# First expert layer: 20 of 32 token tiles go through 48 slot tiles sorted by expert, 12 tiles stay dense

## The chip, the core and the metric

The program runs on one core of a Trainium2 chip. Its engines work side by side and meet at semaphores: PE (TensorE, matmuls; its weight loads are listed as PEld), DVE (VectorE), ACT (ScalarE), POOL (GpSimd) and SP (SyncE, which here only issues DMAs). The metric is the device time of one execution in microseconds, the median over runs. Lower is better.

## The reference, cut to what matters

Six layers follow each other on `x` of 128 x 32 tokens with 128 features. The change concerns the third, the first expert layer. A token's result there is the sum over its two best experts, so the work that the mathematics asks for is 2 of 8 experts for each token:

```python
logits = x @ router_weight                      # 4096 tokens, E = 8 experts
probs = softmax(logits); top_p, top_i = top_k(probs, 2)
top_p = top_p / sum(top_p)
# an expert takes at most cap = ceil(4096 * 2 / 8 * 1.25) = 1280 entries, later ones are dropped
fc1 = gelu(xt @ moe_w1[e])                      # 128 -> 256
fc2 = fc1 @ moe_w2[e]                           # 256 -> 128
moe_out[token] += fc2 * top_p                   # for its two experts
return h1 + moe_out
```

## The kernel before

Tokens lie in 32 tiles of 128 rows (one token in each partition). `k.X` holds the running residual, all in SBUF. Each layer is a stage with its own program for each engine, and all engines meet between stages.

The projection stage (`stage_projection`) ends the attention ahead of the experts: it adds to `k.HID`, normalises rows into `xr`, transposes them into `k.LT` (on ACT, with the layer norm's weight and bias), and makes router logits. POOL adds `k.HID` to `k.X` there (L1583).

The expert stage (`stage_experts_two`) is dense. PE takes blocks of four tiles, and for each block all eight experts: 64 units numbered n = 8 b + e. A unit is `h` (L1654: 2 matmuls of 512 columns), gelu on ACT (L1687), `y` (L1664: 8 matmuls of 128 columns, for four tiles and two halves of the 256), and on DVE four additions into `k.X` scaled with the token's share of that expert, which is zero for the six experts that it doesn't use (L1750). PE runs one `h` ahead of `y`, and y banks are four deep: `y(n)` waits for the additions of unit n-3.

While PE begins, DVE works out the shares in a chain of small operations, each waiting for the one before: softmax, first and second best expert, the number of each entry within its expert (`ranks` on PE, prefix sums over the tiles on DVE, L1729 and L1730), and the drop at 1280. The last of them is L1737; `y(3)` waits for it through the semaphore `known`. After each block DVE takes the row statistics for the next layer norm (L1755, L104). SP and POOL have next to nothing to do in this stage.

The last stage of the program (`stage_routed_experts`) already routes another expert layer, which has one expert for each token, 512 hidden features and a gate. DVE works out a slot for each token (ops up to L2067), POOL stores the normalised rows at their slots in the DRAM tensor `slot_rows` with 32 indirect DMAs (L1853), SP loads 40 slot tiles one at a time into six buffers (L1818), and for each of them PE transposes (L1892), does 8 matmuls (L1900) and 4 more (L1909), ACT does gelu and two copies, DVE copies the expert's first weights (L2013), and POOL stores the result at the tokens' places with an indirect DMA (L1859). PE and DVE read the number of the tile's expert from SBUF into a register of their sequencer (`value_load`, L1905 and L2011).

Of the kernel before, what the change touches and what calls it, by code (L numbers as in the profile page):

```python
# [33 lines left out]
ST = NT + 8  # L34
EPS = 1e-5
# [1441 lines left out]
def stage_projection(nc, k, w, wb, wr):  # L1477
    W = 4
    NG = NT // W
    with ExitStack() as ctx:  # L1480
# [3 lines left out]
        def sem(name):  # L1484
# [7 lines left out]
            "normed", "transposed", "copied", "logits_made", "logits_copied", "x_summed"))  # L1492
        block = ctx.enter_context(nc.Block())
# [4 lines left out]
        def span(g):  # L1498
            return slice(W * g, W * g + W)

        @block.tensor
        def _(pe):
# [6 lines left out]
            def turn(g):  # L1509
                wait(pe, copied, g - 1)  # L1510
                for i in range(W):
                    pe.wait_ge(normed, W * g + i + 1)
                    m = pe.transpose(pT[g % 2][:, i * P:(i + 1) * P], xr[g % 2][:, i, :], k.ident[:, :])
                m.then_inc(turned, 1)
# [35 lines left out]
        def _(dve):  # L1550
# [11 lines left out]
            def norm(g):  # L1562
# [4 lines left out]
                for i, t in enumerate(tiles(g)):  # L1567
                    dve.tensor_scalar(xr[g % 2][:, i, :], k.HID[:, t, :], k.MV[:, t, 0:1], k.RSTD[:, t:t + 1],
                                      ALU.subtract, ALU.mult).then_inc(normed, 1)
# [26 lines left out]
def stage_experts_two(nc, k, low, down, w1, w2):  # L1596
# [4 lines left out]
    NB = NT // TB  # L1601
    with ExitStack() as ctx:
# [12 lines left out]
        pr, tmp, oh, sel = (sb(n, [P, NT, E]) for n in ("probs", "tmp", "onehot", "selected"))  # L1615
        acc = [sb(f"prefix{i}", [P, NT, E]) for i in range(2)]
        pH = (k.bank[0:2], k.bank[2:4])
        WAYS = 4
        pY = k.bank[4:8]
        pR, pC = k.bank[7][:, 0:NT * E], k.bank[7][:, NT * E:2 * NT * E]  # L1620
        ones_set, chain, exped, sel_ready, ranked, shifted, known = (sem(n) for n in (
            "ones_set", "chain", "exp_done", "selected_ready", "ranks_made", "shifted", "shares_known"))
        h_made, gelued, y_made, added, stats = (sem(n) for n in ("h_made", "gelu_done", "y_made", "added", "stats"))
        ctx.callback(leave_stale, k, sems, scope)
        block = ctx.enter_context(nc.Block())

        def blocks(eng, body):

            body(0, True, False)
            with eng.Fori(0, NB - 2) as i:  # L1630
                body(i + 1, False, False)
            body(NB - 1, False, True)

        @block.sync
        def _(sp):
            clear_stale(sp, k)

        @block.gpsimd
        def _(pool):
            pool.memset(ones[:, :], 1.0).then_inc(ones_set, 1)  # L1640

        @block.tensor
        def _(pe):
# [6 lines left out]
            def h(b, e):  # L1650
                n = E * b + e
                wait(pe, gelued, NF * (n - 1))
                for c in range(NF):
                    pe.matmul(pH[e % 2][c][:, :], w1[:, e, c * P:(c + 1) * P], k.LT[:, ts(b, TB), :],  # L1654
                              start=True, stop=True).then_inc(h_made, 1)

            def y(n, e):
                pe.wait_ge(gelued, NF * n + NF)
                wait(pe, added, TB * (n - WAYS + 1))
                if isinstance(n, int) and n == WAYS - 1:  # L1660
                    pe.wait_ge(known, 1)
                for i in range(TB):
                    for c in range(NF):
                        m = pe.matmul(pY[e % WAYS][:, i * D:(i + 1) * D], ge[e % 2][:, c, i * P:(i + 1) * P],  # L1664
                                      w2[:, e, c, :], start=(c == 0), stop=(c == NF - 1))
                m.then_inc(y_made, 1)

            def body(b, first, last):
                for e in range(E):
                    h(b, e)  # L1670
                    if e or not first:
                        y(E * b + e - 1, (e - 1) % E)
                    if first and e == 2:
                        ranks()
                if last:
                    y(E * b + E - 1, E - 1)
            blocks(pe, body)

        @block.scalar
        def _(act):  # L1680
            def body(b, first, last):
                for e in range(E):
                    n = E * b + e
                    wait(act, y_made, n - 1)
                    for c in range(NF):
                        act.wait_ge(h_made, NF * n + c + 1)
                        act.activation(ge[e % 2][:, c, :], pH[e % 2][c][:, :], ACT.Gelu_apprx_tanh)\  # L1687
                            .then_inc(gelued, 1)
# [3 lines left out]
            blocks(act, body)  # L1692

        @block.vector
        def _(dve):
# [16 lines left out]
            first_of(dve, link, tmp[:, :, :], sel[:, :, :], pr[:, :, :], top[:, :], down[:, :])  # L1712

            link(dve.scalar_tensor_tensor(out=k.COMB[:, :, :], in0=sel[:, :, :], scalar=-2.0, in1=pr[:, :, :],
# [3 lines left out]
            first_of(dve, link, tmp[:, :, :], oh[:, :, :], k.COMB[:, :, :], top2[:, :], down[:, :])  # L1718
            dve.tensor_tensor(sel[:, :, :], sel[:, :, :], oh[:, :, :], ALU.add).then_inc(sel_ready, 1)
# [6 lines left out]
            link(dve.tensor_copy(acc[0][:, :, :], pC.rearrange("p (t e) -> p t e", e=E)))  # L1726
            d, a = 1, 0
            while d < NT:
# [3 lines left out]
            link(dve.tensor_tensor(tmp[:, :, :], acc[a][:, :, :], pC.rearrange("p (t e) -> p t e", e=E),  # L1732
                                   ALU.subtract))
            link(dve.tensor_tensor(tmp[:, :, :], tmp[:, :, :], pR.rearrange("p (t e) -> p t e", e=E),
                                   ALU.add))
# [4 lines left out]
            def body(b, first, last):  # L1740
                if last:
# [1025 lines left out]
```

## Time and profile before

| what | value |
|---|---|
| median of 3 runs | 2209.99 us (2206.12 to 2210.51) |
| the profiled execution, its own time | 2209.93 us |
| its span | 2208.1 us |
| TensorE clock granted, mean | 0.973 of 2.4 GHz |
| PE busy | 2061.1 us, 93% |
| DVE busy | 1563.5 us, 71% |
| POOL busy | 1082.8 us, 49% |

Times below are from the span's start. Shares of busy time are means over stages that differ. What counts here is the stretch of the expert stage, 768 to 999 us. The lines called PEldq, DVEq and the like are what an engine's sequencer did itself: reading a register, computing an address, waiting for a semaphore.

### The profile page before, as it was taken

The page shows a single profiled execution, that of the slowest core. Times are in us where ns is not written, and L with a number is a line of the kernel's source. Part 1 is how long each engine was busy: PE and PEld are TensorE (multiplying, and loading weights), DVE is VectorE, ACT ScalarE, POOL GpSimd, SP SyncE. Part 2 cuts the span into 40 slices and gives each one's busy share as a digit, 9 for nine tenths or more (in the row PEclk, how much of TensorE's full clock was granted, in tenths as well). Part 3 has the DMA queues.
Part 4 walks back from the last instruction along what each step waited for, and adds up shares of the span by engine and source line. Part 5 has one row for each costly group of instructions (what it writes and reads, how often), then busy time and mean ns, then how long its engine had stood idle before and what let it go on. Part 6 is the DMA issues. An engine that isn't in the chain of part 4 may idle for free. (4 is left out here: it accounts for less than half of the span.)

```text
span 2208.1 us, 80213 instructions
## 1 busy us (share of the span) xinstructions
PE 2061.1 (93%) x27341; PEld 1519.6 (69%) x27342; DVE 1563.5 (71%) x5619; ACT 1271.6 (58%) x3620; POOL 1082.8 (49%) x1119
## 2 busy tenths in 40 slices
PE   8899999997999899997999999999889999989998
PEld 5577777774677677775777777777555666666897
DVE  6888888874777743336988999988866667764444
ACT  5555555555888433334777777777645555542332
POOL 2233434433888300005777777777356666643332
PEclk9999999997999899997999999999999999988999
DMA  6620000000000000001111111111140000000113
GB/s 216 208 65 0 0 0 0 0 1 1 1 0 0 1 1 0 0 0 40 38 36 36 36 37 46 37 36 36 34 179 0 0 0 0 0 2 26 40 47 99
DMA packets 37290, 71.69 MB, mean 32 GB/s; under 512 B 6048, under 2 KB 25504, under 8 KB 36512
## 3 DMA queue, kind: packets, MB, share of 16 engines
q1 hardware_dynamic: 34896, 65.78, 9.4%
q0 software_dynamic: 2304, 4.74, 0.7%
q8 instruction: 53, 0.87, 0.2%
q14 instruction: 37, 0.30, 0.0%
HBM read 63.67 MB, written 9.47 MB: 33 GB/s over the span
## 5 line engine op out<-in xcount | busy, mean ns | idle before, releaser
L2343 ACT ACTIVATE xat_scores<-xat_scores,xat_least 128x257 f32<-128x257 f32 x512 | 258.5, 505 | 84.2 <-DVE xat_least L2484 84.0
L2484 DVE CUSTOM_DVE_ANT_0 xat_scores<-bank,xat_mask_b 128x257 f32<-128x257 f32 x512 | 203.1, 420 | 51.6 <-PE bank L2189 45.0
L1107 POOL TENSOR_TENSOR gqa_rnorm<-gqa_norm_min,gqa_minus_half 128x12 f32<-128x12 f32 x64 | 145.8, 2278 | 103.9 <-DVE gqa_norm_min L1184 103.9
L2245 PE MATMUL bank<-ident,xat_scores 128*128 128x128 f32 x1024 | 189.5, 288 | 0.3 <-DVE xat_p_T L2491 0.2
L751 POOL TENSOR_TENSOR lin_q_softmax<-lin_q_exp,lin_q_rsum 128x512 f32<-128x512 f32 x64 | 66.7, 1042 | 223.2 <-DVE lin_q_rsum L812 223.2
L2245 PEld LDWEIGHTS bank<-ident,xat_scores 128*128 128x128 f32 x1024 | 116.0, 141 | 81.9 <-issue 43.8
L1750 DVE SCALAR_TENSOR_TENSOR X<-bank,expert_shares,X 128x128 f32 (+1 forms) x256 | 72.2, 344 | 130.7 <-PE bank L1664 130.4
L1687 ACT ACTIVATE moe_gelu<-bank 128x512 f32<-128x512 f32 x128 | 76.3, 597 | 146.2 <-PE bank L1654 146.2
L1425 POOL TENSOR_TENSOR bat_scores<-bat_scores,bat_max 128x512 f32<-128x512 f32 x128 | 130.4, 1040 | 32.6 <-DVE bat_max L1457 32.6
L1664 PEld LDWEIGHTS bank<-moe_w,moe_gelu 128*128 128x128 f32 x1024 | 124.2, 192 | 30.8 <-issue 18.4
L1457 DVE CUSTOM_DVE_ANT_0 bat_scores<-bank,bat_causal_add 128x128 f32<-128x128 f32 x512 | 110.7, 286 | 47.1 <-PE bank L1313 47.1
L629 PEld LDWEIGHTS bank<-lin_w_v_out,lin_z_T 128*128 128x128 f32 x1024 | 119.1, 191 | 22.0 <-issue 20.2
L629 PE MATMUL bank<-lin_w_v_out,lin_z_T 128*128 128x128 f32 x1024 | 131.2, 281 | 1.3 <-ACT lin_z_T L681 1.3
L1664 PE MATMUL bank<-moe_w,moe_gelu 128*128 128x128 f32 x1024 | 124.6, 275 | 0.3 <-DVE expert_shares L1737 0.3
L1654 PE MATMUL bank<-ln_T,moe_w 128*128 (+1 forms) x256 | 122.9, 604 | 0.8 <-PEq L1480 0.8
L2356 ACT ACTIVATE xat_p_T<-bank 128x256 f32<-128x256 f32 x256 | 96.2, 376 | 47.0 <-PE bank L2245 40.2
L2389 POOL TENSOR_TENSOR xat_p_rsum_wide<-xat_p_rsum,xat_head_of_row 128x128 f32<-128x128 f32 x128 | 51.2, 400 | 146.6 <-DVE xat_p_rsum L2497 146.6
L2430 POOL TENSOR_SCALAR xat_keep<-xat_pad 128x1028 f32<-128x1028 uint8 x1 | 1.5, 1545 | 237.5 <-DMA xat_pad<-in_xat_pad 237.5
L2491 DVE COPY xat_p_T<-bank 128x256 f32<-128x256 f32 x256 | 106.6, 417 | 0.3 <-PE bank L2245 0.2
L2189 PE MATMUL bank<-xat_k_cos,xat_q_blocks 32*128 32x257 f32 x1024 | 92.7, 431 | 7.5 <-DVE xat_least L2484 3.0
L2343 ACT ACTIVATION_READ_ACCUMULATOR xat_scores<-xat_scores,xat_least 128x1 f32 x512 | 97.6, 191 | 0.0
L1054 ACT ACTIVATE gqa_squares<-bank 128x512 f32<-128x512 f32 x64 | 38.2, 597 | 90.8 <-PE bank L917 90.7
(324 smaller groups left out, 5876.5 us busy)
## 6 DMA issues: line engine op xcount, KB each, us to landing
glu_ctx_N<-in_ctxN SPq DMA_DIRECT2D x32, 576.0 KB, 3.7
xat_ctx_T<-in_ctxT SPq DMA_DIRECT2D x32, 516.0 KB, 3.6
xat_pad<-in_xat_pad SPq DMA_DIRECT2D x32, 128.5 KB, 3.3
expert_w<-in_glx_w SPq DMA_DIRECT2D x1, 4096.0 KB, 14.9
slot_rows<-in_empty_rows SPq DMA_DIRECT2D x1, 2580.0 KB, 9.9
slt_rows<-slot_rows SPq DMA_DIRECT2D x40, 64.5 KB, 1.8
moe_w<-in_moe_w SPq DMA_DIRECT2D x2, 1024.0 KB, 6.0
expert_w<-in_glx_w SPq DMA_DIRECT2D x1, 2048.0 KB, 19.3
```

What stands on the lines that cost most here:

```text
L629: m = pe.matmul(pY[:, 0:D], zT[slot][:, hd, :], wvo[:, hd // 2, hd % 2, :], start=(hd == 0), stop=(hd == H - 1))
L1107: pool.tensor_tensor(rn[h][:, :], sm[h][:, :], half_neg[:, :], ALU.pow).then_inc(rnorm, 1)
L1425: pool.tensor_tensor(sx[g][:, :, :], sx[g][:, :, :], spread(mx[g][:, :], P), ALU.subtract).then_inc(s_shifted, 1)
L1457: dve.tensor_tensor_reduce(sx[g][:, i, :], pS[g][:, i * P:(i + 1) * P], cadd[:, :], 1.0, -BIG, ALU.add, ALU.max, mx[g][:, i:i + 1]).then_i ...
L1654: pe.matmul(pH[e % 2][c][:, :], w1[:, e, c * P:(c + 1) * P], k.LT[:, ts(b, TB), :], start=True, stop=True).then_inc(h_made, 1)
L1664: m = pe.matmul(pY[e % WAYS][:, i * D:(i + 1) * D], ge[e % 2][:, c, i * P:(i + 1) * P], w2[:, e, c, :], start=(c == 0), stop=(c == NF - 1))
L2189: m = pe.matmul(pS[g][:, 0:J], qb[slot][r, part, j, :, :], keys[j % 2][r, :], start=(part == 0), stop=(part == 1))
L2245: m = pe.transpose(dst[:, c * P:(c + 1) * P], sx[j % 2][:, g, c * P:(c + 1) * P], k.ident[:, :])
L2343: act.activation(sx[j % 2][:, g, :], sx[j % 2][:, g, :], ACT.Exp, bias=mn[j % 2][g][:, 0:1], scale=-1.0, accum_out=sm[j % 2][:, g:g + 1]). ...
L2356: act.activation(pt[j % 2][g][:, :], unit_bank(*at)[:, 0:NC * P], ACT.Copy).then_inc(pa_copied, 1)
L2484: dve.tensor_tensor_reduce(sx[j % 2][:, g, :], pS[g][:, 0:J], mb[slot][:, j, :], 1.0, BIG, ALU.add, ALU.min, mn[j % 2][g][:, 0:1]).then_in ...
L2491: dve.tensor_copy(pt[j % 2][g][:, :], unit_bank(*at)[:, 0:NC * P]).then_inc(pd_copied, 1)
```

## The change

The last 12 tiles stay dense (`DENSE` are blocks 5, 6 and 7), two of their blocks (`EARLY`) ahead of the slot tiles and one behind. The first 20 tiles (`NR`) are routed. The projection stage keeps their normalised rows in two copies (`kept`), one for each choice; POOL makes the second. In the expert stage DVE also works out a slot for each of a token's two entries; POOL writes for each an expanded row (128 features, the share, and the place of the result) into the DRAM tensor `moe_rows`: 2 x 20 indirect DMAs. Each expert's entries begin at a multiple of 128, so that each of 48 slot tiles (`NS` = 2 x 20 + 8) has one expert, whatever the data. All 48 are worked through, also those that stay empty.

For each slot tile SP loads the rows into one of 8 buffers, PE transposes them, ACT copies them out of PSUM with weight and bias, PE multiplies with 128 x 256 weights that DVE has copied out (2 matmuls), ACT does gelu, PE multiplies with the second weights straight from `w2` (2 matmuls), DVE scales with the share that came with the row, and POOL stores at the token's place in `moe_results` with an indirect DMA. At the end SP loads the two sets of results over `k.HID` and `k.AT`, POOL adds the pairs, and DVE adds the sum to `k.X` (`join`) and takes statistics. Ahead of the stage, among the early loads of the second stage, `moe_rows` is filled from a host array of 6144 x 130.

```diff
+NR = 20
+NS = 2 * NR + 8
 def stage_projection(nc, k, w, wb, wr, kept):
+                if g < KEPT:
+                    pool.wait_ge(normed, W * g + W)
+                    pool.tensor_copy(kept[1][:, span(g), 0:D], kept[0][:, span(g), 0:D]).then_inc(doubled, 1)
 def stage_experts_two(...):
+    DENSE = tuple(range(NR // TB, NT // TB))
+    EARLY = 2
+    WAYS, OUTS = 8, 4
         def _(sp):
+            sp.wait_ge(scattered, 16 * 2 * NR)
+            def again(before, t, slot, stores):
+                sp.wait_ge(turned, before + 1)
+                sp.wait_ge(stored[slot % OUTS], 16 * stores)
+                sp.dma_start(xr[slot][:, :], rows[ts(t, P), :]).then_inc(landed[slot], 16)
...
         def _(pool):
+            for c in range(2):
+                pool.wait_ge(slots_known, c + 1)
+                for t in range(NR):
+                    pool.indirect_dma_start(rows, ...slots[c][:, t:t + 1]..., kept[c][:, t, :], None)
+            def body(t, slot):
+                pool.wait_ge(y_scaled, t + 1)
+                pool.sem_inc(pool_waited, 1)
+                pool.indirect_dma_start(results, ...xr[slot]...PLACE..., yo[slot % OUTS][:, :], None)
         def _(pe):
+            def body(t, slot):
+                if not ends_at(t):
+                    transpose(t + 1, (slot + 1) % WAYS)
+                slot_h(t, slot)
+                if not begins(t):
+                    slot_y(t - 1, (slot - 1) % WAYS)
+            dense(range(EARLY), True)
+            pe.wait_ge(gelued, NF * E * EARLY)
+            pe.wait_ge(added, TB * E * EARLY)
+            pe.wait_ge(tiles_known, 1)
+            tiles(pe, body)
+            pe.wait_ge(y_scaled, NS)
+            dense(range(EARLY, len(DENSE)), False)
         def _(dve):
+            def body(t, slot):
+                if not ends_at(t):
+                    pick(t + 1, (slot + 1) % WAYS)
+                if not begins(t):
+                    y_scale(t - 1, (slot - 1) % WAYS)
```

In PE's program a dense unit stood, inside the loop over blocks, as here (of before; L1654 is `h`, L1664 is `y`):

```order
L1654 MATMUL bank<-ln_T,moe_w 128x512 x2
L1664 MATMUL bank<-moe_w,moe_gelu 128x128 x8
```

Between the second and the third of the dense blocks PE now has 48 slot tiles; one of them, inside the loop, reads as follows (of the change; L1767 is the transpose, L1774 `slot_h`, L1779 the reading of the expert's number, L1783 `slot_y`):

```order
L1767 MATMUL bank<-ident,moe_slot_row 128x128 [waits moe_xT_copied,moe_rows_landed4]
L1770 REGISTER_ALU
L1774 MATMUL bank<-moe_slot_xT,moe_picked_w 128x128 [waits moe_slot_gelu_done,moe_w1_picked,moe_xT_copied]
L1774 MATMUL bank<-moe_slot_xT,moe_picked_w 128x128
L1779 ISA
L1779 TENSOR_LOAD moe_tile_expert
L1779 ISA x2
L1783 ISA [waits moe_y_scaled,moe_slot_gelu_done]
L1783 MATMUL bank<-moe_w,moe_slot_gelu 128x128
L1783 ISA
L1783 MATMUL bank<-moe_w,moe_slot_gelu 128x128
```

Five short matmuls stand where ten stood in a unit, and seven steps of the sequencer stand among them.

On DVE, the end of the chain at the start of the stage was this (of before; L1737 is what `y(3)` waits for, L1750 the first additions):

```order
L1732 TENSOR_TENSOR moe_tmp<-moe_prefix,bank 128x256
L1734 TENSOR_TENSOR moe_tmp<-moe_tmp,bank 128x256
L1736 TENSOR_SCALAR moe_tmp<-moe_tmp 128x256
L1737 TENSOR_TENSOR expert_shares<-moe_probs,moe_tmp 128x256
L1750 SCALAR_TENSOR_TENSOR X<-bank,expert_shares,X 128x128 x32
```

Now 13 operations stand ahead of the same point (L1881 to L1893, of which the last ones are shown), and 13 more between it (L1896) and the first additions (L1924):

```order
L1893 TENSOR_TENSOR moe_spot<-moe_tmp,moe_tokens_of 128x160
L1895 TENSOR_SCALAR moe_tmp<-moe_tmp 128x256
L1896 TENSOR_TENSOR expert_shares<-moe_probs,moe_tmp 128x256
L1899 TENSOR_TENSOR moe_picked_spot<-moe_spot,moe_onehot 128x160
L1900 TENSOR_REDUCE moe_slot_float<-moe_picked_spot 128x20
L1901 TENSOR_TENSOR moe_picked_spot<-expert_shares,moe_onehot 128x160
L1902 TENSOR_REDUCE moe_rows_kept<-moe_picked_spot 128x20
L1903 CAST moe_slot<-moe_slot_float 128x20
```

The additions of all dense blocks are later by all of these operations; POOL's indirect DMAs can begin after the first of the two L1903.

At the end of the stage DVE's program is this (of the change; L1951 is `join`, L1913 and L106 are the statistics, L1924 the additions of the last dense units). Before, a block ended with its 32 additions and 4 of each statistic:

```order
L1924 SCALAR_TENSOR_TENSOR X<-bank,expert_shares,X 128x128 x20
L1951 TENSOR_TENSOR X<-X,hidden 128x1024
L1913 BN_STATS bn_stats<-X 128x6 x8
L106 BN_AGGR mean_var<-bn_stats 128x2 x8
L1924 SCALAR_TENSOR_TENSOR X<-bank,expert_shares,X 128x128 x4
L1951 TENSOR_TENSOR X<-X,hidden 128x1024
```

The joins stand between the additions of the last four dense units.

## Rows read from the trace of the kernel before

**Rows 1.** The page's first part: busy time and share of the span.

```profile
PE 2061.1 (93%) x27341; PEld 1519.6 (69%) x27342; DVE 1563.5 (71%) x5619; ACT 1271.6 (58%) x3620; POOL 1082.8 (49%) x1119
```

**Rows 2.** Groups by line in 768 to 999 us: count, busy, mean, idle before.

```profile
L1664 PE MATMUL bank<-moe_w,moe_gelu 128*128 128x128 f32 x1024 | 124.6, 275 | 0.3 <-DVE expert_shares L1737 0.3
```

**Rows 3.** Timeline of PE early in the stage: start, length, line, count.

```profile
785.95 2.02 PE L1664 MATMUL bank<-moe_w,moe_gelu 128*128 128x128 f32 x16 [0.32 <-DVE expert_shares L1737]
...
789.53 1.95 PE L1664 MATMUL bank<-moe_w,moe_gelu 128*128 128x128 f32 x16
...
793.03 1.95 PE L1664 MATMUL bank<-moe_w,moe_gelu 128*128 128x128 f32 x16
```

**Rows 4.** Timeline of DVE in the chain.

```profile
783.16 0.36 DVE L1730 TENSOR_TENSOR moe_prefix<-moe_prefix 128x192 f32<-128x192 f32 x1
783.55 0.23 DVE L1729 COPY moe_prefix<-moe_prefix 128x128 f32<-128x128 f32 x1
...
785.38 0.43 DVE L1737 TENSOR_TENSOR expert_shares<-moe_probs,moe_tmp 128x256 f32<-128x256 f32 x1
```

**Rows 5.** Timeline of DVE in the last stage's chain.

```profile
2008.17 0.17 DVE L2051 TENSOR_TENSOR top_ends<-top_ends 128x7 f32<-128x7 f32 x1
2008.37 0.17 DVE L2050 COPY top_ends<-top_ends 128x2 f32<-128x2 f32 x1
...
2012.46 0.49 DVE L2063 TENSOR_TENSOR top_tiles_past<-top_ends,counts 128x320 f32<-128x320 f32 x1
```

**Rows 6.** The indirect stores L1853 (first and last start), then SP's timeline after them.

```profile
L1853 POOL DMA_INDIRECT slot_rows<-rows_normed,slot_of_token x32: 954/958/1215, 2014.9 to 2054.3; - x32
```

```profile
2058.12 2.70 SPq L1818 DMA_DIRECT2D slt_rows<-slot_rows  x6
```

**Rows 7.** PE's sequencer in a slot tile: L1905 load, L1909 addresses, L57 waits.

```profile
L1905 PEldq TENSOR_LOAD <-expert_of_tile x1: 302/302/302, 2101.0 to 2101.0; - x1
...
L1909 PEldq FUSED_REGOPS  x4: 46/46/46, 2101.8 to 2102.1; - x4
...
L57 PEldq EVENT_SEMAPHORE  x3: 51/51/51, 2101.7 to 2102.5; - x3
```

**Rows 8.** Timeline of DVE, and of POOL at the end of the slot tiles.

```profile
2100.31 0.69 DVE L2024 TENSOR_TENSOR slt_gh_T<-slt_gelu,bank 128x512 f32<-128x512 f32 x1 [1.13 <-PE bank L1900]
2101.36 0.69 DVE L2013 COPY slt_w<-expert_w 128x1024 f32 x1 [0.37 <-issue]
```

```profile
2180.25 0.96 POOL L1859 DMA_INDIRECT token_results<-slt_y,slt_rows  x1 [1.72 <-ACT slt_y L1962]
2181.51 0.96 POOL L1859 DMA_INDIRECT token_results<-slt_y,slt_rows  x1 [0.30 <-issue]
```

**Rows 9.** Stretches: length, busy (count) of PE PEld DVE ACT POOL, granted clock, DMA.

```profile
733.00:757.00 24.00, 17.74 (x180) 15.25 (x180) 19.66 (x92) 7.38 (x14) 8.89 (x7) 0.98 0.00 1
757.00:768.00 11.00, 9.48 (x44) 9.05 (x45) 5.58 (x25) 2.81 (x6) 1.30 (x2) 0.50 0.00 0
...
1979.00:2003.00 24.00, 23.22 (x106) 20.19 (x106) 11.31 (x39) 10.70 (x34) 0.39 (x2) 0.52 0.00 1
2068.00:2180.00 112.00, 111.51 (x997) 111.36 (x998) 54.90 (x80) 42.28 (x118) 36.45 (x38) 1.00 0.15 43
```

**Rows 10.** Timeline of DVE at the stage's end.

```profile
996.50 1.12 DVE L1750 SCALAR_TENSOR_TENSOR X<-bank,expert_shares,X 128x128 f32<-128x128 f32 x4 [0.66 <-PE bank L1664]
997.65 0.87 DVE L1755 BATCH_NORM_STATS2 bn_stats<-X 128x6 f32<-128x128 f32 x4
998.56 0.38 DVE L104 BATCH_NORM_AGGREGATE mean_var<-bn_stats 128x2 f32<-128x6 f32 x4
```

**Rows 11.** Timeline: fetching results in the last stage (SP, DVE), POOL's sums in the projection.

```profile
2183.80 2.51 SPq L1839 DMA_DIRECT2D results_by_token<-token_results  x5
...
2192.30 1.22 DVE L2008 TENSOR_TENSOR X<-X,results_by_token 128x1024 f32<-128x1024 f32 x1
```

```profile
743.73 1.27 POOL L1583 TENSOR_TENSOR X<-X,hidden 128x512 f32<-128x512 f32 x1 [1.74 <-DVE hidden L1553]
```

More of the change, by code:

```diff
@@ L1663, in y @@
                     for c in range(NF):
-                        m = pe.matmul(pY[e % WAYS][:, i * D:(i + 1) * D], ge[e % 2][:, c, i * P:(i + 1) * P],
-                                      w2[:, e, c, :], start=(c == 0), stop=(c == NF - 1))
+                        m = pe.matmul(pY[e % BANKS][:, i * D:(i + 1) * D], ge[e % 2][:, c, i * P:(i + 1) * P],
+                                      w2[:, (e * NF + c) * D:(e * NF + c + 1) * D], start=(c == 0), stop=(c == NF - 1))
                 m.then_inc(y_made, 1)
[L1668 to L1676, printed above, removed]
@@ L1677, in _, with dense, transpose @@
-            blocks(pe, body)
+            def dense(some, ranking):
+                for i in some:
+                    for e in range(E):
+                        n = E * i + e
+                        h(n, DENSE[i], e)
+                        if e or i != some[0]:
+                            y(n - 1, (e - 1) % E)
+                        if ranking and i == 0 and e == 2:
+                            ranks()
+                y(E * some[-1] + E - 1, E - 1)
+            def transpose(t, slot):
+                pe.wait_ge(landed[slot], 16 * (turns(t, slot, WAYS) + 1))
+                wait(pe, xt_ready, t - 1)
+                pe.transpose(pX[slot % 2][:, 0:P], xr[slot][:, 0:D], k.ident[:, :]).then_inc(turned, 1)
@@ L1679, in _, with dense @@
+            pe.wait_ge(tiles_known, 1)
+            tiles(pe, body)
+            pe.wait_ge(y_scaled, NS)
+            dense(range(EARLY, len(DENSE)), False)
         @block.scalar
         def _(act):
[L1681 to L1688, printed above, removed]
+            def dense(some):
+                for i in some:
+                    for e in range(E):
+                        n = E * i + e
+                        wait(act, y_made, n - 1)
+                        for c in range(NF):
+                            act.wait_ge(h_made, NF * n + c + 1)
+                            act.activation(ge[e % 2][:, c, :], pH[e % 2][c][:, :], ACT.Gelu_apprx_tanh).then_inc(gelued, 1)
@@ L1690, in _ @@
             act.wait_ge(shifted, 1)
             act.activation(pr[:, :, :], pr[:, :, :], ACT.Exp).then_inc(exped, 1)
-            blocks(act, body)
+            dense(range(EARLY))
+            tiles(act, body)
+            dense(range(EARLY, len(DENSE)))
         @block.vector
@@ new lines, in _ @@
+            for i in range(EARLY):
+                for e in range(E):
+                    take(i, e)
+            dve.wait_ge(tiles_known, 1)
+            tiles(dve, body)
+            lo, mid, hi = NR, TB * DENSE[EARLY], NT
+            dve.wait_ge(added, TB * E * EARLY)
+            look(lo, mid)
+            for i in range(EARLY, len(DENSE)):
+                for e in range(E):
+                    take(i, e)
+                    if i == len(DENSE) - 1 and 4 <= e < 4 + len(GROUPS):
+                        join(e - 4, *GROUPS[e - 4])
```

241 lines of the change are left out of this document (190 added, 51 removed).

## The prediction, made blind

> **What bounds the kernel now.** I read the page's first part, then the groups by line of the expert stage, then its timeline. PE is busy 93% of the span [rows 1], and in this stage all of it: its 1024 records of `y` make 124.6 us and before them PE sat idle for 0.3 us in all [rows 2]. A dense unit follows the last at 3.50 us, read between two starts of `y` [rows 3]. ACT and DVE wait for PE in each unit, so the stage is as long as PE's work, from 768 to 998.94 us, where the last statistic ends [rows 10]. Only one thing else shows: `y(3)` starts at 785.95, right behind L1737, which ends at 785.81 [rows 3, 4]. What shortens PE's stream here shortens the program, until something else is last.
>
> **What is removed.** 20 of 32 tiles leave the dense loop: 5 blocks x 8 units x 3.505 us = 140.2 us of PE.
>
> **Early dense blocks.** DVE's chain gets longer. A small operation costs 0.20 us from start to start [rows 5], one of 128 x 192 costs 0.39 [rows 4], so I take 0.37 for 128 x 160, and for 128 x 384 0.62 (0.49 at 128 x 320, scaled, with the gap) [rows 5]. Ahead of the shares stand ten small ones and three of 128 x 160: 10 x 0.20 + 3 x 0.37 = 3.1 us, so the shares are known at 788.9. Then for each choice 4 x 0.37 + 0.22 = 1.7 us, twice, and 2 x 0.62 + 0.22 for the experts of tiles: DVE is free at 793.8, the first additions end about 794.95, and `y(4)`, which stood at 789.53, waits for them. After that units run at 3.505 again: `y(14)` at 830.0, and `y(15)`, which has no `h` ahead of it, ends at 833.6. The loss against the old course is 5.4 us.
>
> **Scattering the rows.** POOL can start after the first slots, at 790.6. It stood idle in the stage, so nothing is queued behind it but its own stores. The nearest rows are the 32 stores of the last stage, 2014.9 to 2054.3, thus 1.27 us each; 65 KB in each, as here [rows 6]. With the 0.95 us that pass there before the first: 791.6 + 39 x 1.27 = 841.1 for the last start. SP's first load followed the last start there by 3.8 us (2054.3 to 2058.12) [rows 6], and I take 2.0 us for landing: PE transposes the first slot tile at 846.9. So PE sits idle for 13.3 us. Nothing hides this, since the third dense block is put behind the slots.
>
> **One slot tile.** Work of the array: 5 matmuls of 128 columns at full speed, about 1.0 us (a `y` of 8 takes 1.95 less the drain) [rows 3]. POOL: 0.96 busy and 0.30 between two in a row, 1.26 us, also in the tile loop when two results wait [rows 8]. But PE's sequencer does its own steps in between. In the last stage's tile the register load starts at 2101.0, the first address step of `y` comes at 2101.8, four of these run to 2102.1, and the last wait ahead of the next `h` is at 2102.5 [rows 7]. With 0.1 us for the step ahead of the load that is 1.6 us; two address steps fewer save 0.25, and sending out the matmuls of `slot_h` adds 0.15 to 0.25. I take 1.6 us. There it costs nothing, as 12 matmuls keep the array busy for 111.5 of 112 us [rows 9]; here 5 matmuls are no cover. DVE needs from one instruction over its register load to the copy 1.05 us (2100.31 to 2101.36) [rows 8], and with a copy of a quarter the size and a scaling some 1.45: near to PE's, a little below. Bounds: 1.26 (PE's queue hides the steps, POOL is last) and 2.81, the period of the last stage, if handovers set it (997 matmul records in 112 us at 25 for each tile [rows 9]).
>
> **The clock.** PE has been idle 13 us when slots start. In the rows the clock stood at its lower level (1.2 GHz) for the 11 us ahead of the stage, behind a projection where PE was busy 17.74 of 24 us at 0.98, and for 24 us from 1979 though PE was busy in 23.22 of them [rows 9]. So I let the first 20 us of slots run at 1.2 GHz, where five matmuls take 1.95 to 2.0 us: 10 tiles. In the rest the array works about 0.6 of the time, less than in the projection, and I add 1.5 us for more of the same.
> The Trainium skill (TensorE: Matmul & The Clock Gate, A second HAM failure mode) warns of a clock that swings between its two levels where PE idles shortly between groups of matmuls; that speaks against this change, and the trace's projection agrees with it; its worst is the rival "half clock" below.
>
> Slots together: 1.1 us until the first `slot_h`, 10 x 1.98 + 38 x 1.6 + 1.5 = 82.1 us, and 2 us from the last `slot_y` to the scaled result that PE waits for. The last dense block starts at S = 846.9 + 85.2 = 932.1.
>
> **The end.** PE's block ends at S + 28. Fetching: the last store's start to SP's first load of results was 2.3 us (2181.51 to 2183.80), and a sum was ready to start 8.5 us later [rows 8, 11]. Here 2.6 MB come in six loads; even with 17 us and POOL's pair sums (2 x 1.27 us for 8 tiles [rows 11]) the pairs are there by S + 18. `y` of the fifth unit ends at S + 19.2, and then DVE is last: additions 1.12, a join of 8 tiles 1.22, statistics of 8 tiles 2 x 0.87 and 2 x 0.38, with gaps 5.0 us for a unit with a join [rows 10, 11] against 3.5 of PE. Additions and joins: S + 24.3, 29.3, 32.0 (four tiles), the eighth unit 33.1, statistics of its tiles S + 34.4 = 966.5.
>
> **Sum.** 998.9 - 966.5 = 32.4 us less. In parts: -140.2 dense, +5.4 chain, +13.3 idle, +85.2 slots, and +4 because the end is DVE's (PE to end was 2.5 us, now 6.4). These give -32.3. POOL's five copies in the projection lie in its idle 1.74 us of each group [rows 11], and if one doesn't fit, DVE and PE don't wait for it. I cost them at nothing, the fill of `moe_rows` (3.2 MB among loads at the start of the second stage) at nothing too, since no one needs it before 790 us; if either shows it is 1 us, which I put in: -31. The profiled execution took 2209.93 us with a span of 2208.1 and its time is the median of the runs to 0.1 us. Predicted: **2179 us**.
>
> **Rivals.**
> *Overlap is better* (chance 0.13): PE's queue takes in the next tile while its sequencer loads. For it: there, the steps are hidden. Against it: there the queue was full, here it runs empty. 38 tiles at 1.26: 13 us less, 2166.
> *Half clock* (0.17): the array, which works 0.6 of the time, never gets 2.4 GHz back until the dense block: 38 x 0.38 less the 1.5 counted = 13 us, and up to 10 us in the first 20 us of the dense block: 2192 to 2202. For it the 24 us at 0.52 with a busy PE; against it most stretches with pauses, which run at 1.0 [rows 9].
> *Handovers set the pace, slower* (0.09): slot buffers come free only when their result has landed (SP waits for `stored`), DVE's copy waits for PE's `h` and its scaling for `y`. If that kept the last stage's 2.81 us per tile, slots take 135 us: 2179 + 53 = 2232. It ends slower than before from 2.25 us per tile. Against it: the buffer's way (load 2.0, two tiles' time, 1.2 to scaling, 0.8 to POOL, 2.3 to landing and SP) is about 6.9 us + 2 periods, under the 8 periods that eight buffers give.
> *Stores in a row* (0.03): the 40 stores don't overlap. Each takes 2.3 us from its start until SP can go on [rows 8, 11]: 40 x 2.3 = 92 instead of 50.5, 41 us more, 2220. The 1.27 us [rows 6] speak against it.
> The Trainium skill (DMA: Bandwidth & Descriptors, Anatomy of one DMA, SWDGE path) gives about 2.0 us and bytes / 436e3 for each DMA from GpSimd: taken as a cost in series that is this rival; the trace disagrees, with 1.27 us from one to the next.
>
> **How the numbers follow.** The likeliest has 0.58. Below 2163 I see 0.04, above 2202 the last two rivals with 0.12: the range is 2163 to 2202. Within 0.2% (4.4 us, about what a measurement of this kernel can tell) only the third rival near its break-even falls: 0.02. Faster 0.88, slower 0.10.
>
> **What would show it.** Right: `y(3)` at 789 and `y(4)` at 795; 40 stores at 1.27 us from 791.6; PE's gap of 13 us; slot tiles at 1.6 us with PE's sequencer, not a semaphore, ahead of `slot_y`; a lower clock at their start; DVE last at the end. Wrong: a period other than 1.6 us per tile: each 0.1 us is 4.8 us.

## The result, and the profile after

The changed kernel took **2174.84 us** (median of 4 runs, 2173.39 to 2176.83) against 2210.25 us (4 runs, 2206.12 to 2212.77) of the kernel before on the same chip: ratio 0.9842, 95% interval 0.9825 to 0.9859, so 35.4 us faster. Later runs on a chip numbered 6 gave 2173.00 against 2211.86 us (7 runs), ratio 0.9827 (0.9807 to 0.9847). There the kernel was run four times; one execution, at 2309.47 us with a granted clock of 0.829, was disturbed and is left out of both figures.

The page's first part, as [rows 1]:

```profile
span 2171.6 us, 80082 instructions
...
PE 1991.1 (92%) x26973; PEld 1477.1 (68%) x26974; DVE 1559.5 (72%) x5584; ACT 1261.6 (58%) x3636; POOL 1177.0 (54%) x1217
```

PE has 70.0 us less work on a span 36.5 us shorter (2208.1 before). The timeline of PE where the early dense blocks end and the slot tiles begin, to be laid beside [rows 3]:

```profile
830.59 3.73 PE L1749 MATMUL bank<-moe_w,moe_gelu 128*128 128x128 f32 x32
846.24 0.92 PE L1767 MATMUL bank<-ident,moe_slot_row 128*128 128x128 f32 x2 [11.92 <-DMA moe_slot_row<-moe_rows]
...
848.25 0.42 PE L1767 MATMUL bank<-ident,moe_slot_row 128*128 128x128 f32 x1
848.47 1.06 PE L1774 MATMUL bank<-moe_slot_xT,moe_picked_w 128*128 128x128 f32 x4
...
850.17 0.42 PE L1767 MATMUL bank<-ident,moe_slot_row 128*128 128x128 f32 x1
...
852.09 0.32 PE L1767 MATMUL bank<-ident,moe_slot_row 128*128 128x128 f32 x1
```

The gap ends with the landing of the first rows. From 848.25 a tile comes every 1.92 us, while each group of four matmuls takes 1.06 us; from 852 the groups take 0.61. The windows view says the same (length, busy and count of PE, PEld, DVE, ACT, POOL, granted clock, DMA share, GB/s):

```profile
834.00:846.00 12.00, 0.32 (x3) 0.13 (x2) 1.62 (x6) 0.00 (x0) 6.79 (x8) 0.69 0.17 52
846.00:852.00 6.00, 5.68 (x24) 5.13 (x25) 0.99 (x3) 2.87 (x7) 0.42 (x1) 0.50 0.32 73
852.00:924.00 72.00, 60.60 (x410) 49.84 (x409) 29.27 (x91) 37.03 (x89) 43.73 (x47) 1.00 0.29 79
```

POOL's two rows of stores (durations in ns, first and last start), the scatter's to be read beside [rows 6]:

```profile
L1715 POOL DMA_INDIRECT moe_rows<-moe_rows_kept,moe_slot x40: 954/958/1215, 792.5 to 842.0; - x40
...
L1721 POOL DMA_INDIRECT moe_results<-moe_slot_y,moe_slot_row x48: 953/957/1016, 851.6 to 925.2; - x48
```

The first are 49.5 / 39 = 1.27 us apart, the second 73.6 / 47 = 1.57 us. The 1.57 is a mean. Most tiles come near 1.5 us, but some take 1.8 to 2.0, among them, in every eight, the two where the loop over the eight buffers branches back (L1666, on which PE's sequencer spends 871.7 to 872.2); here those that begin at 870.47 and 872.33:

```profile
870.47 0.27 PE L1767 MATMUL bank<-ident,moe_slot_row 128*128 128x128 f32 x1
...
872.33 0.30 PE L1767 MATMUL bank<-ident,moe_slot_row 128*128 128x128 f32 x1
...
874.20 0.27 PE L1767 MATMUL bank<-ident,moe_slot_row 128*128 128x128 f32 x1
```

What PE and DVE do for two ordinary tiles:

```profile
887.18 0.27 PE L1767 MATMUL bank<-ident,moe_slot_row 128*128 128x128 f32 x1
887.29 0.61 PE L1774 MATMUL bank<-moe_slot_xT,moe_picked_w 128*128 128x128 f32 x4
888.12 0.71 PE L1783 MATMUL bank<-moe_w,moe_slot_gelu 128*128 x4 [0.22 <-DVE moe_slot_y L1936]
888.66 0.27 PE L1767 MATMUL bank<-ident,moe_slot_row 128*128 128x128 f32 x1
888.86 0.68 PE L1774 MATMUL bank<-moe_slot_xT,moe_picked_w 128*128 128x128 f32 x4
889.84 0.71 PE L1783 MATMUL bank<-moe_w,moe_slot_gelu 128*128 x4 [0.29 <-issue]
```

```profile
887.56 0.35 DVE L1936 TENSOR_SCALAR moe_slot_y<-bank,moe_slot_row 128x128 f32<-128x128 f32 x1 [0.78 <-PE bank L1783]
888.47 0.29 DVE L1931 COPY moe_picked_w<-moe_w 128x256 f32 x1 [0.56 <-PE bank L1774]
889.02 0.35 DVE L1936 TENSOR_SCALAR moe_slot_y<-bank,moe_slot_row 128x128 f32<-128x128 f32 x1 [0.26 <-PE bank L1783]
```

DVE copies the next tile's weights at 888.47, PE's `slot_h` follows at 888.86, `slot_y` at 889.84 with "issue" ahead of it (its own sequencer). That PE waits for the copy shows only in its sequencer: the step that waits for it (L59) begins at 888.5 and takes 0.29 us, until the copy ends; the same step of the next tile, at 890.2, takes 0.05. Where PE itself sat idle between 852 and 924, it was ahead of `slot_y`, and 8.2 of 10.5 us are its own steps:

```profile
L59 PEldq EVENT_SEMAPHORE  x1: 292/292/292, 888.5 to 888.5; - x1
```

```profile
L1783 PE MATMUL bank<-moe_w,moe_slot_gelu 128*128 x186 | 33.1, 301 | 10.5 <-issue 8.2 <-DVE moe_slot_y L1936 2.1
```

At the end of the stage, as [rows 10] before:

```profile
924.23 3.70 PE L1739 MATMUL bank<-ln_T,moe_w 128*128 128x512 f32 x8 [0.45 <-DVE moe_slot_y L1936]
...
961.13 0.47 PE L2438 MATMUL bank<-ident,xat_xn 128*128 128x128 f32 x1 [8.61 <-DVE xat_xn L2670]
```

```profile
953.80 0.68 DVE L1951 TENSOR_TENSOR X<-X,hidden 128x512 f32<-128x512 f32 x1
...
957.75 0.38 DVE L106 BATCH_NORM_AGGREGATE mean_var<-bn_stats 128x2 f32<-128x6 f32 x4
```

DVE ends at 958.13, 40.8 us ahead of 998.94. The span gained 36.5, so 4.3 us were lost behind the stage. The first statistic of the attention stage's output still comes 41.0 us earlier (1052.1 before, 1011.1 after), the last one, at the end of the stages between, 36.4 (1975.1 and 1938.7). They go in steps; one is this pause inside a group of 64 equal matmuls, which the kernel before did not have there:

```profile
1921.89 1.25 PE L964 MATMUL bank<-gqa_v_ones,gqa_p 32*32 32x65 f32 x60
1924.65 0.30 PE L964 MATMUL bank<-gqa_v_ones,gqa_p 32*32 32x65 f32 x4 [1.51 <-issue]
```

### The profile page after: what moved, and what is told of

Its sections match the earlier page's. It is cut to its first block and busy times, and to the rows that moved or that the text cites. A ratio compares the mean times of both kernels' runs of the same rounds, so it can differ in the third digit from the quotient of the medians.

```text
span 2171.6 us, 80082 instructions
## 1 busy us (share of the span) xinstructions
PE 1991.1 (92%) x26973; PEld 1477.1 (68%) x26974; DVE 1559.5 (72%) x5584; ACT 1261.6 (58%) x3636; POOL 1177.0 (54%) x1217
## 5 line engine op out<-in xcount | busy, mean ns | idle before, releaser
L1382 ACT ACTIVATE bat_p_T<-bank 128x512 f32<-128x512 f32 x128 | 76.1, 594 | 24.8 <-PE bank L1323 24.8
L1323 PEld LDWEIGHTS bank<-ident,bat_scores 128*128 128x128 f32 x512 | 54.9, 142 | 50.9 <-ACT bat_scores L1377 25.3
L1323 PE MATMUL bank<-ident,bat_scores 128*128 128x128 f32 x512 | 77.4, 285 | 12.7 <-ACT bat_scores L1377 12.7
L2070 POOL DMA_INDIRECT token_results<-slt_y,slt_rows x40 | 38.8, 969 | 88.5 <-ACT slt_y L2173 88.2
L704 ACT ACTIVATE lin_q_T<-bank 128x512 f32<-128x512 f32 x64 | 38.2, 597 | 79.8 <-PE bank L594 79.8
L2409 PE MATMUL bank<-xat_ctx_kept,xat_w_k 128*128 128x257 f32 x256 | 78.4, 388 | 6.4 <-POOL xat_ctx_kept L2617 6.4
## 6 DMA issues: line engine op xcount, KB each, us to landing
slot_rows<-in_empty_rows SPq DMA_DIRECT2D x1, 2580.0 KB, 10.4
```

Source lines behind the costliest of these rows:

```text
L1323: m = pe.transpose(pT[g % 2][:, i * P:(i + 1) * P], sx[g][:, i, :], k.ident[:, :])
L2409: pe.matmul(pK[:, 0:J], wk[:, :], ck[slot][:, j, :], start=True, stop=True).then_inc(k_made, 1)
```

## Experiments on chips like the first

All four of this section ran on chip 6; differences are to the changed kernel there, 2173.00 us.

**The changed kernel again** (no edit).

> The changed kernel itself, unaltered, to have its trace beside others on one chip. The four experiments before this one ran on another chip than the kernel before and the changed one had: there the kernel before takes 2240.3 us, not 2210.3, and in the first of them PE has a gap of 25.43 us (824 to 850 us) while POOL issues its 40 stores of rows, which the changed kernel's own trace does not have. Theory A (the gap belongs to the chip and comes with any row of such stores): on such a chip the changed kernel has that gap twice, here and in the last expert layer, which the kernel before has once; the change then gives 35 us less some 30 to 36, a ratio between 0.995 and 1.003. On a chip like the first there is no gap and the ratio is 0.984 again. Theory B (the gap came from the edits of those experiments): no gap in this run on any chip, ratio 0.984.

Measured 2173.00 us and PE's gap is 11.90 us, as in the first trace. Its slots take 849.03 to 926.74 = 77.7 us (78.0 there). Why this run was wanted is told in the next section; on this chip its question does not arise.

**Both lookups away.** Expert 0's weights serve all slot tiles on PE and DVE, so this leaves out the choice of expert.

```diff
-                e = pe.value_load(tile_expert[0:1, ts(t, 1)], min_val=0, max_val=E - 1)
...
-                                  w2[:, bass.ds(e * F + c * D, D)], start=(c == 0), stop=(c == NF - 1))
+                                  w2[:, c * D:(c + 1) * D], start=(c == 0), stop=(c == NF - 1))
...
-                e = dve.value_load(tile_expert[0:1, ts(t, 1)], min_val=0, max_val=E - 1)
-                dve.tensor_copy(we[slot % 2][:, :], w1[:, ts(e, F)]).then_inc(picked, 1)
+                dve.tensor_copy(we[slot % 2][:, :], w1[:, 0:F]).then_inc(picked, 1)
```

> Slot tiles with the weights of expert 0 for every tile (no lookup on PE or DVE; so the results of the slot tiles are not the layer's), to be read against the changed kernel on the same chip. Theory A (PE and DVE wait for each other in a loop that the two lookups lengthen): the 48 slot tiles go from 1.57 us each to the pace of POOL's stores, 1.27 us, so 48 x 0.30 = 14 us less than the changed kernel. Theory B (POOL's stores or their landing set the pace already): under 3 us less. Theory C (gelu and copy on ACT or the array set it): under 6 us less.

Measured 2161.03 us (2157.0 to 2163.5), ratio to the kernel before 0.9772 (0.9755 to 0.9789): 12.0 us less than the changed kernel, nearest to theory A's 14. PE's timeline shows tiles 1.28 us apart in the mean (880.40 to 886.80, five tiles):

```profile
884.18 0.33 PE L1767 MATMUL bank<-ident,moe_slot_row 128*128 128x128 f32 x1
...
885.52 0.33 PE L1767 MATMUL bank<-ident,moe_slot_row 128*128 128x128 f32 x1
...
886.80 0.33 PE L1767 MATMUL bank<-ident,moe_slot_row 128*128 128x128 f32 x1
```

The slot tiles, from the first transpose to the next dense block, take 847.58 to 913.57 = 66.0 us, not 77.7. From 869.80 to 907.73 POOL starts 31 stores 1.26 us apart, with 0.30 us between two, the pace of a row of stores:

```profile
874.86 0.95 POOL L1721 DMA_INDIRECT moe_results<-moe_slot_y,moe_slot_row  x1 [0.30 <-issue]
876.12 0.96 POOL L1721 DMA_INDIRECT moe_results<-moe_slot_y,moe_slot_row  x1 [0.30 <-DVE moe_slot_y L1934]
```

So POOL is then the bound, and the array is not: early in the row this run's tiles at 853.41, 854.41 and 855.41 came 1.00 us apart.

**Joins on GpSimd.** GpSimd adds the paired results to X too.

```diff
+                pool.wait_ge(paired, g + 1)
+                pool.tensor_tensor(k.X[:, lo:hi, :], k.X[:, lo:hi, :], k.HID[:, lo:hi, :], ALU.add).then_inc(joined, 1)
...
-                dve.wait_ge(paired, g + 1)
-                dve.tensor_tensor(k.X[:, lo:hi, :], k.X[:, lo:hi, :], k.HID[:, lo:hi, :], ALU.add).then_inc(joined, 1)
```

> GpSimd adds the paired results to X itself, DVE only takes the statistics. Theory A (the end of the stage is DVE's queue of three additions of 8, 8 and 4 tiles behind the last dense unit): DVE ends some 5 us behind the last dense unit now; without the three additions, of some 1.5 to 2.5 us each, the stage ends 2 to 5 us earlier, ratio to the changed kernel 0.998. Theory B (GpSimd's additions are late, at its slower rate of 3.57 us for 8 tiles, and DVE waits for them): no difference or up to 2 us slower.

Measured 2169.98 us, 0.9818 (0.9801 to 0.9834) to before: 3.0 us less than the changed kernel, within theory A's 2 to 5, but the two intervals overlap, so the times alone don't show it; the trace must bear it. From the start of the last dense block to the next stage's first matmul it is 922.78 to 956.98 = 34.2 us, against 36.9 of the changed kernel (926.74 to 963.63 on this chip, 924.23 to 961.13 in the first trace): 2.7 us at the place named. GpSimd takes 2.35 us for eight tiles, not 3.57 (that figure was of two additions in one row):

```profile
938.57 2.35 POOL L1728 TENSOR_TENSOR X<-X,hidden 128x1024 f32<-128x1024 f32 x1
```

**20 dense units ahead, joins on GpSimd.** The loop over dense work goes by unit: 20 ahead of the slot tiles, 4 behind.

```diff
-    EARLY = 2
+    UNITS = 20
...
-            dense(range(EARLY), True)
+            dense(range(UNITS), True)
...
-            dense(range(EARLY, len(DENSE)), False)
+            dense(range(UNITS, E * len(DENSE)), False)
```

> The run of the joins on GpSimd, with four more dense units (a unit: one expert on one block of four tiles) ahead of the slot tiles and four fewer behind them. Theory A: in the changed kernel PE has nothing to do for 11.92 us between its last dense unit and the first rows landed; four units of 3.5 us (14.0 us) lie in that gap, so the slot tiles begin some 2 us later and 14.0 us of dense work behind them are gone: 12 us less than the joins alone, less what the clock does. Only four units are then behind the slot tiles, 14 us, while the results' loads, pair sums and additions take from 927.7 to about 942 in the changed kernel (14 us): the joins become the end, which takes some 4 us back, so 8 us less in all. Theory B (on a chip where PE has its own 25 us gap during the stores): the gap is not filled, and the gain is under 3 us.

Measured 2170.03 us, 0.9816 (0.9799 to 0.9832) to before: equal to the joins alone and 3.0 us less than the changed kernel, where 8 us less than the joins alone were expected. The gap is filled, and the slots begin at 848.46 and take 75.9 us, at a clock of 1.00 throughout. But the stage no longer follows PE:

```profile
934.93 3.73 PE L1751 MATMUL bank<-moe_w,moe_gelu 128*128 128x128 f32 x32
955.00 0.48 PE L2436 MATMUL bank<-ident,xat_xn 128*128 128x128 f32 x1 [16.34 <-DVE xat_xn L2668]
```

PE is idle for 16.34 us at the end, 5.90 us in the joins alone: of the 14.0 us that left its block, 10.4 come back as waiting for the results' way home (loads at 927.7, first pair sum 932.69, DVE's last statistic 949.1). And ACT begins the next stage's table load only at 952.28, where in the joins alone it followed DVE by 0.3 us. GpSimd's last addition ends at 944.75, but the instruction that ends its block (DRAIN, from 943.5) takes 8.58 us, up to 952.0, and all engines go on at 952.2: that is the end here.

```profile
L1617 POOLq DRAIN  x1: 8577/8577/8577, 943.5 to 943.5; - x1
```

Behind that the clock, windows of this run and then of the joins alone:

```profile
943.00:955.00 12.00, 0.00 (x0) 0.00 (x0) 6.69 (x40) 1.60 (x2) 1.68 (x2) 0.50 0.00 1
955.00:980.00 25.00, 14.91 (x75) 9.60 (x75) 11.28 (x31) 7.92 (x25) 16.47 (x10) 0.50 0.18 58
980.00:993.00 13.00, 12.39 (x144) 9.36 (x144) 11.10 (x47) 9.38 (x33) 5.53 (x6) 0.98 0.01 1
```

```profile
955.00:971.00 16.00, 5.71 (x25) 3.42 (x25) 6.51 (x12) 2.51 (x5) 8.92 (x6) 0.50 0.27 91
971.00:993.00 22.00, 19.40 (x211) 14.15 (x209) 18.37 (x78) 17.34 (x63) 14.61 (x13) 0.99 0.07 19
```

PE stood for 16.3 us and not 5.9, and the 1.2 GHz level lasted until 980, not 971. From the stage's first matmul to its first output statistic it takes 52.1 us (955.00 to 1007.1) and not 48.1 (956.98 to 1005.1): 4.0 us given back, against 2.0 gained.

That the longer rest is the reason isn't shown, and other runs speak against it. The changed kernel and the run with both lookups away rest equally long there, 8.61 and 8.60 us, but the low level lasts 20.8 us from the first matmul in the one and 25.5 in the other, and the way to the first output statistic is 50.0 and 52.2 us; the kernel before, after 5.49 us, needed 50.2. Of these six traces the joins alone have the shortest way, 48.1, so about half of the 4.0 us, and part of what the joins alone gained, is that run's luck.

```profile
961.13:981.90 20.77, 10.77 (x50) 6.60 (x51) 9.93 (x25) 5.54 (x16) 13.93 (x8) 0.50 0.21 70
```

```profile
950.47:976.00 25.53, 15.51 (x77) 10.01 (x78) 11.47 (x32) 7.92 (x25) 16.48 (x10) 0.50 0.17 58
```

## Experiments on chips where the core stands during the stores

The other eight ran on two chips, 12 and 14, where the kernel before takes 2240.30 us (9 runs) and 2239.32 us (31 runs), 27 to 30 us more than in the runs above. The changed kernel itself was not run there.

**20 dense units alone**, the edit above without the joins:

> The same work in another place: 20 dense units (two and a half blocks) run ahead of the slot tiles and 4 behind, in place of 16 and 8. Theory: PE's gap of 12 us before the first slot tile is filled with dense units, the slots start 1 to 2 us later, and 14 us of dense work are gone behind them; the results are fetched about 14 us after the last slot tile, so the end is that fetch and DVE's joins. 8 to 12 us less than the changed kernel, 2163 to 2167 us. Rival: the joins and the fetch, which were hidden, take it all back: no change, 2172 to 2176 us.

Measured 2248.06 us on chip 12, ratio 1.004 (1.0027 to 1.0053): slower than before. PE's timeline shows what none of the runs above has:

```profile
813.35 3.20 PE L1749 MATMUL bank<-moe_w,moe_gelu 128*128 128x128 f32 x14 [5.51 <-issue]
...
825.34 1.01 PE L1739 MATMUL bank<-ln_T,moe_w 128*128 128x512 f32 x1 [1.09 <-issue]
851.79 3.79 PE L1749 MATMUL bank<-moe_w,moe_gelu 128*128 128x128 f32 x16 [25.44 <-ACT moe_gelu L1813]
```

Some 14 us into POOL's scatter (794.1 to 843.6) PE stops, then does a few matmuls, and from 826 nothing, until 851.79. In the last stage, which the kernel before has too, the same comes again in its 32 stores:

```profile
2046.41 2.08 PE L2086 MATMUL bank<-shared_w,glx_gh 128*128 128x128 f32 x8 [9.84 <-DVE glx_gh L2207]
...
2067.35 2.07 PE L2086 MATMUL bank<-shared_w,glx_gh 128*128 128x128 f32 x8 [15.45 <-DVE glx_gh L2207]
```

**One lookup or both away**, one execution each on chip 12 (expert 0 for every slot tile where a lookup is gone; edits as above, by half and whole).

> PE no longer reads the expert's number in a slot tile: the second matmuls always take the weights of expert 0, so the results of the routed tiles are other numbers. In the changed kernel the 48 slot tiles took 77.0 us from the first slot_h (847.2) to the first matmul of the last dense block (924.2), 1.57 us each at 2.4 GHz. Theory A, PE's sequencer alone sets the period: without 0.8 us of steps DVE is next, about 1.45 us each, slots 70 to 71 us. Theory B, a loop over DVE and PE sets it (DVE's register load and copy follow the scaling, PE's next slot_h waits for the copy): DVE's part stays, 1.4 to 1.5 us each, slots 69 to 73 us. Theory C, POOL or the array: no change, 77 us. The time falls by what the slots lose, 2168 to 2170 under A and B.

> DVE no longer reads the expert's number: it always copies the first weights of expert 0, so the results of the routed tiles are other numbers; PE's load stays. Theory A, PE's sequencer alone: no change, 1.57 us each, slots 76 to 78 us. Theory B, the loop over DVE and PE: PE's own steps remain, which between two waits make 1.43 us, slots 69 to 72 us. Theory C, POOL or the array: no change.

> Neither PE nor DVE reads the expert's number; both always take the weights of expert 0, so the results of the routed tiles are other numbers. Theories A and B: POOL's stores are the next bound at 1.26 us each, slots 61 to 64 us. Theory C, POOL or the array is the bound already: no change, 77 us. If semaphore latency around the ring of tiles is what counts, between: 66 to 72 us.

Single runs of 2245.18, 2241.87 and 2238.23 us beside 2240.30 of before. All three have the gap (25.43, 25.41, 22.63 us in the longest piece). Nothing on the lookups follows: the 48 stores of results take 83.4, 79.2 and 81.7 us from first to last start, longer than the 73.6 of the changed kernel with its lookups. One thing does follow: the edit with both lookups away and that with 20 units ahead ran on chip 6 too, without the gap, so it does not come from the edits but goes with the chip or the time of the runs.

**One lookup away, again**, with repeated runs, on chip 14.

> Expert 0's second weights for every slot tile on PE, without PE's lookup of the expert (so the slot tiles' results are not the layer's); DVE's lookup stays. With both lookups gone the changed kernel was 13.2 us faster. Theory A (PE's own instructions, the lookup and the address worked out from it, are the longer half of the loop): 8 to 13 us less than the changed kernel (2174.5 us on the chip of that run). Theory B (DVE's lookup and copy are): under 4 us less.

> Expert 0's first weights copied for every slot tile on DVE, without DVE's lookup (so the slot tiles' results are not the layer's); PE's lookup stays. Theory A (PE's half of the loop is the longer): under 4 us less than the changed kernel. Theory B (DVE's): 8 to 13 us less. If both runs are 4 to 8 us less, the two lookups lie one behind the other in one loop, and each is paid in full.

Measured 2237.03 us (0.9984, 0.9973 to 0.9995) and 2239.30 us (1.0003, 0.9988 to 1.0017) against before. Inconclusive: they do not share a chip with the changed kernel, and their result stores take 81.5 and 79.8 us from first to last start. Which lookup costs more stays open.

**Picks three tiles ahead**, and then with 20 dense units. Four buffers of picked weights, nothing left out:

```diff
-        we = [sb(f"picked_w1{i}", [P, F]) for i in range(2)]
+        we = [sb(f"picked_w1{i}", [P, F]) for i in range(4)]
...
-                wait(dve, th_made, t - 1)
+                wait(dve, th_made, t - 3)
...
-                    pick(t + 1, (slot + 1) % WAYS)
+                    pick(t + 3, (slot + 3) % WAYS)
...
```

> Four buffers for the picked first weights and the pick three tiles ahead, not two buffers and one tile. Nothing is left out. Theory A (PE and DVE wait for each other once a tile because the pick can only begin when PE has used the buffer before): PE's wait of 0.29 us per tile for the pick goes, the tile falls from 1.57 to about 1.45 us (PE's own instructions and DVE's each come to 1.43 to 1.46 us), 48 x 0.12 = 6 us less than the changed kernel. Theory B (the engines' own instructions set the tile's time already, the wait is what is left over): no change beyond 1 us.

> The picks three tiles ahead, with 20 dense units ahead of the slot tiles and 4 behind, and the additions to X left on DVE. The run with 20 units and the additions on GpSimd gained nothing over the additions alone: its stage ended 2 us earlier, held to 952 us by GpSimd's end of block (8.58 us behind its last addition), and the clock was half for 37 us behind it, not 17. Theory A (GpSimd's end was the block's end there): with the additions on DVE the stage ends 2 to 3 us earlier than that, so at 949 us less what the picks save, and the time is that of the picks alone less 2 to 6 us. Theory B (what is gained at the stage's end is lost again to the clock in the stage behind it, some 4 us): equal to the picks alone within 2 us.

Measured 2240.87 us (0.9997, 0.9987 to 1.0007) and 2242.91 us (1.0009, 0.9993 to 1.0025) on chip 14. The first is the nearest to the changed kernel that ran there, and no change against before can be seen. For the first run's theories the changed kernel is missing there; the second is 2.0 us slower, where 2 to 6 us faster (theory A) or equal within 2 us (B) was expected, but with the gap in both it says nothing on the stage's end. The first run's DVE and ACT in the stretch of the 40 stores:

```profile
803.21 1.13 DVE L1924 SCALAR_TENSOR_TENSOR X<-bank,expert_shares,X 128x128 f32<-128x128 f32 x4 [5.87 <-PE bank L1749]
831.98 1.13 DVE L1924 SCALAR_TENSOR_TENSOR X<-bank,expert_shares,X 128x128 f32<-128x128 f32 x4 [27.64 <-issue]
846.83 2.16 DVE L1924 SCALAR_TENSOR_TENSOR X<-bank,expert_shares,X 128x128 f32<-128x128 f32 x8 [13.73 <-remote]
```

```profile
807.44 0.60 ACT L1815 ACTIVATE moe_gelu<-bank 128x512 f32<-128x512 f32 x1 [1.45 <-remote]
838.35 0.60 ACT L1815 ACTIVATE moe_gelu<-bank 128x512 f32<-128x512 f32 x1 [30.31 <-issue]
```

The account of where the 35 us went on chip 14, from this run's trace: its slots start at 871.49, not 846.24, 25.3 us later, and its next dense block's first statistic is at 954.7, not 924.1: 30.6 us in this stage. From the scatter's first store to the last result store in the last stage it takes 195.2 us (2014.4 to 2209.6); the kernel before took 166.6 on the first chip (2014.9 to 2181.5). These 28.6 us fit what the kernel before pays as well on chip 14 (2239.3 less 2210.3 is 29.0; no trace of it there was kept), so they would cancel in the ratio; the 30.6 are new with the change and eat most of its gain. The rest is in part between the first and the last statistic of the stages between, 931.5 us here and 927.6 in the changed kernel.

What holds the engines is open. The stores themselves are not slower: 1.27 us apart and 0.96 us long in both. What differs in the records is that the landing times of this stage's 88 indirect stores and of the loads between them are missing from these traces, which the first chip's have (2.3 and 2.2 us in the middle). This trace has 4477 landing records and 18321 of semaphore updates, the changed kernel's 6569 and 20551, so what the rows above name as the end of a wait is uncertain. A rival that I did not try: the recording itself. The Trainium skill (NOTIFIC — the notification-queue block, Overflow: three behaviours, one of which stalls the engine) says that a full record queue can, by its setting, either lose records or stall what produces them. The setting is one for each queue there, so a single queue would do one or the other; missing records and standing engines together would need queues that are set differently. If it were so, the loss would be one of profiled executions on such chips; no run here shows which it is.

## Why the prediction was right, by its steps

Predicted 2179 us, measured 2174.84; forecast 31 us less, measured 35.4. The mechanism came as forecast; that the number is this close is in part luck, as two errors cancel in half (see "Behind the stage").

- *Chain:* `y(3)` at 789, measured 790.02, behind `expert_shares` as said; `y(4)` at 795, measured 795.48; units at 3.50 us. The stage itself began 1.5 us later (769.51, 768.00 before), as if for the 1 us put in; but the runs on chip 6, with the same code ahead, begin it between 767.47 and 772.55, so this doesn't show that term.
- *Scatter:* 40 stores 1.27 us apart from 791.6, measured 792.5; first transpose at 846.9, measured 846.24; PE's idle time 13.3, measured 11.92.
- *Slot tile:* taken as 1.6 us, set by PE's sequencer. The whole row came at 1.57. That the lookups lengthen it is shown (12.0 us by taking both away); that PE's alone does is not. The rows have a loop, in which DVE waits for `slot_h` and in some tiles PE for DVE's copy; PE's own steps explain most of its idle time (8.2 of 10.5 us), as predicted, but the 1.43 to 1.46 us of own steps on either side are an estimate of mine, and no run that could settle it ran beside the changed kernel. The longer tiles where the loop branches back were not in the prediction; they are part of its 1.57.
- *Clock:* the term that was mis-sized. Ten tiles at 1.98 us and 1.5 us for more of the same were predicted; three tiles at 1.92 came. Of the 85.2 us for the slots 78.0 were needed: 7.2 less. The clock's part is 7 tiles at 0.38 and the 1.5, 4.2 us; the rest is the pace, 1.57 for 1.6 on the tiles at full speed (1.4), and beginning and end (1.6). The swing that the prediction feared did not come in the slots: PE is busy 60.60 of 72 us with a short pause in each tile, at 1.00. Nor do the projection's rows show one, as the prediction had it: 0.98 over 24 us and 0.50 over 11 [rows 9] are one fall. The run with no low clock in the slots needed 75.9 us, so the low clock costs 2.1 us at most.
- *End:* S + 34.4 predicted, S + 33.9 measured (924.23 to 958.13), with DVE last as said. The joins on GpSimd confirm the place (2.7 us in the trace).
- *Behind the stage:* costed at nothing, but 4.3 us were lost, in later stages whose code is unchanged. These two errors, 7.9 us too late at S and 4.3 us too little behind, cancel in half, which is luck. The run with both lookups away has no loss between the first and the last statistic (922.9 us, as before's 923.0; the changed kernel's are 927.6 and, on chip 6, 926.9, the two others there 928.1 and 928.4), but it loses 2 us ahead of the first (52.2 us from the stage's first matmul, 50.2 before). So the loss doesn't belong to the slot tiles as such; the cause is open, one 1.51 us pause for "issue" apart.
- *Rivals:* half clock, handovers and stores in a row did not come. "Overlap is better" named the floor rightly, POOL's 1.26 us, but PE's queue doesn't reach it with the lookups in.

What the prediction did not have at all is the chip: it names no rival by which the change gains 35 us on one chip and, in its nearest variant (picks ahead), nothing on another.

## What to carry to other kernels

Work in short tiles with a weight chosen at run time is paid by the lookup and the handover it puts in the loop, 12.0 us over 48 tiles here (0.25 us of 1.57), before the array matters; count them per tile first. Before dense work is moved into a gap, ask what follows the last of it: here 14 us moved ahead made PE wait 10.4 us longer for the results' way home. Before a few microseconds are put down to an edit, see how the same stretch varies where nothing was changed: the way to the next stage's first statistic was 48 to 52 us in six traces. Measure a change that adds rows of indirect stores on more than one chip, and read each experiment against the parent kernel on its own chip.

## What the runs showed of the hardware that was not expected

- On chips 12 and 14, and not on chip 6 or in the first runs, a row of 40 indirect stores at 1.27 us came with PE standing for 22 to 28 us in one piece, and ACT and DVE with it.
- The instruction that ends GpSimd's block took 8.58 us in both runs with the joins there and 9.64 in the changed kernel, each time up to 7.3 us behind the end of GpSimd's last addition; it is hidden unless GpSimd works up to the stage's end.
- The granted clock at the slots' start was low for 6 us after PE's first matmul there, PE busy 5.68 of them, behind a rest of 11.92 us. In the next stage it stayed low for 20.8 and for 25.5 us behind two rests of 8.6 us, PE busy 10.77 and 15.51 of them, and for 25 behind one of 16.34 us: the length of the rest does not tell how long the low level lasts.
